# Attention and mixture of experts on one core: the order inside an attention step, the routing chain and the expert loops

## The reference

```python
def xattn(x, context, Wq, Wk, Wv):          # x is layernorm(x)
    q = x @ Wq.T
    k_raw, v_raw = context @ Wk.T, context @ Wv.T
    kv = jnp.concatenate([k_raw, v_raw], -1).reshape(b, m, 32, 16, 2)
    k, v = kv[..., 0].transpose(0, 2, 1, 3), kv[..., 1].transpose(0, 2, 1, 3)
    q, k = rmsnorm(q heads), rmsnorm(k)
    attn = softmax(einsum('bhnd,bhmd->bhnm', q, k) * 16 ** -0.5)
    return einsum('bhnm,bhmd->bhnd', attn, v)   # back to (b, n, 512)

def ffn(x, ...):                            # x is layernorm(x)
    gate = x @ Wr + br
    ids = top_k(gate + gate_bias, 2)
    probs = softmax(gate over the two chosen, -inf elsewhere)
    u = x @ Wup[e] + bup[e]                 # for each of 7 routed experts
    g = silu(u @ Wgate[e] + bgate[e]) * u
    out = sum_e probs[e] * (g @ Wdown[e] + bdown[e])
    return out + the same form with the shared expert's weights

x = x + xattn(layernorm(x), ctx, ...)
x = x + ffn(layernorm(x), ...)
```

## Time and profile before

| | us |
|---|---|
| median of 3 runs | 982.45 |
| range of the runs | 982.33 to 983.61 |
| the profiled execution | 984.33 |
| its span | 982.6 |
| busy: PE / PEld | 952.8 (97%) / 685.5 (70%) |
| busy: DVE / ACT / POOL | 707.1 (72%) / 497.6 (51%) / 203.3 (21%) |
| granted TensorE clock, mean | 0.992 |
| DMA | 86.28 MB, mean 88 GB/s |

### The profile page before, as it was taken

How to read it: one execution, slowest core, us unless ns; L and a number is a source line. 1 busy time by engine, 2 the same in 40 slices (tenths; PEclk the granted TensorE clock), 3 DMA queues, 4 the chain that set the end, 5 groups by cost and what they waited for, 6 DMA issues and landing times.

```text
span 982.6 us, 18038 instructions
## 1 busy us (share of the span) xinstructions
PE 952.8 (97%) x6720; PEld 685.5 (70%) x6721; DVE 707.1 (72%) x1460; ACT 497.6 (51%) x619; POOL 203.3 (21%) x209
## 2 busy tenths in 40 slices
PE   7999999999999999999999999999999999999995
PEld 6633443454443553345989998999989999999995
DVE  6798667876778757885968985855857576858653
ACT  4588568866787568887333222422424243424221
POOL 1011000311012200321100000333233333233331
PEclk9999999999999999999999999999999999999998
DMA  9400100100201020223411242543644536635523
GB/s 331 163 1 22 65 1 1 44 33 12 86 2 43 38 71 1 83 79 102 189 66 44 75 156 97 159 109 53 177 83 103 143 76 190 183 66 152 120 52 41
DMA packets 32217, 86.28 MB, mean 88 GB/s; under 512 B 7712, under 2 KB 7712, under 8 KB 28064
## 3 DMA queue, kind: packets, MB, share of 16 engines
q1 hardware_dynamic: 21632, 59.65, 16.9%
q0 software_dynamic: 10528, 25.87, 13.1%
HBM read 61.83 MB, written 23.67 MB: 87 GB/s over the span
## 4 chain that ended last, share of the span: by engine, by line
PE 85%; DVE 10%; issue 2%; DMA 1%; ACT 1%; DVEq 0%; POOLq 0%; SPq 0%; POOL 0%; ACTq 0%
PE z_ps L875 16%; PE y_ps L875 15%; PE u_ps L875 15%; PE o_ps L611 10%; PE scores L595 7%; PE bank_b L632 5%; PE bank_a L648 4%; PE bank_b L618 2%; PE xt_ps L887 2%; PE bank_a L618 2%; PE tr L671 2%; PE tr L666 1%; PE tr L677 1%; DMA ctx_raw<-ctx_t 1%; DVE k_lo L1390 1%
## 5 line engine op out<-in xcount | busy, mean ns | idle before, releaser
L1144 ACT ACTIVATE probs<-scores 128x2048 f32<-128x2048 f32 x128 | 240.7, 1880 | 77.6 <-PE scores L595 74.6
L875 PE MATMUL z_ps<-u_hi,w_sb 128*128 128x256 f32 x896 | 167.9, 285 | 1.4 <-DVE u_lo L1819 1.4
L875 PE MATMUL u_ps<-x_hi,w_sb 128*128 128x256 f32 x864 | 159.4, 283 | 3.0 <-issue 3.0
L1174 ACT ACTIVATE u_hi<-u_ps,b_ug 128x256 fp32r<-128x256 f32 x108 | 45.4, 471 | 199.9 <-PE u_ps L875 199.9
L875 PEld LDWEIGHTS z_ps<-u_hi,w_sb 128*128 128x128 f32 x896 | 140.6, 190 | 2.7 <-DVE u_lo L1819 1.8
L875 PE MATMUL y_ps<-w_sb,g_hi 128*128 128x512 f32 x448 | 139.5, 392 | 0.0
L875 PEld LDWEIGHTS u_ps<-x_hi,w_sb 128*128 128x128 f32 x864 | 135.5, 190 | 5.5 <-issue 4.5
L611 PE MATMUL o_ps<-probs,v_sb 128*17 128x512 f32 x1024 | 136.4, 605 | 0.0
L875 PE MATMUL z_ps<-u_lo,w_sb 128*128 128x256 f32 x448 | 126.3, 282 | 0.0
L875 PE MATMUL u_ps<-x_lo,w_sb 128*128 128x256 f32 x432 | 121.9, 282 | 0.0
L1186 ACT ACTIVATE s_sb<-z_ps,b_ug 128x256 f32<-128x256 f32 x112 | 47.1, 472 | 105.7 <-PE z_ps L875 105.7
(11 more groups left out here) (246 smaller groups left out, 1579.6 us busy)
## 6 DMA issues: line engine op xcount, KB each, us to landing
w_raw<-w_all SPq DMA_DIRECT2D x27, 1024.0 KB, 6.9
ctx_raw<-ctx_t SPq DMA_DIRECT2D x4, 1024.0 KB, 7.3
out<-x_sb SPq DMA_DIRECT2D x16, 256.0 KB, 2.0
x_sb<-x SPq DMA_DIRECT2D x1, 3072.0 KB, 16.2
xn<-x_t SPq DMA_DIRECT2D x12, 256.0 KB, 4.4
xn_dram<-xn SPq DMA_DIRECT2D x12, 256.0 KB, 2.1
xt_dram<-xt SPq DMA_DIRECT2D x6, 512.0 KB, 3.0
xg<-xt_dram POOLq DMA_DIRECT2D x10, 256.0 KB, 3.2
```

The costliest lines, as they stand in the source:

```text
L875: ins = nc.tensor.matmul(out_ps, stat[a], mov[b], start=(first and a + b == 0), stop=(last and a == 1), skip_group_check=True)
L1144: nc.scalar.activation(probs[:, t % 2], scores[:], ACT.Exp).then_inc(p_ready, 1)
L1174: last = nc.scalar.activation(u_hi[:, c, :], u_ps[:, b, a, :], ACT.Identity, bias=b_ug[:, par, 0, c:c + 1])
```

## The change

1. `weighed(t-1)` comes directly behind `scored(u, s)`, `between` and `after` behind it.
2. In units 2, 6 and 10 `sum_k(u + 1)` moves from `between` of step 2 to `after`, behind v_even; DVE's v_out moves ahead of its sums_k accordingly.
3. PE, ACT and DVE run the seven experts unrolled in Python (`experts`), each with its tile loop; the seven bounds are loaded once into registers, on PE in the y phase of tiles 5 and 6, on ACT and DVE in during_y of tile 7. SP and POOL keep `routed`.
4. SP loads the weights of expert 2 in three pieces (`load_weight`), behind output tiles 5, 13 and 15.
5. One of the splits of the shared expert's down weights goes to ACT (`first_weight_high(2, 3)`, step 7 of unit 13), and DVE's neighbouring ones move: (2,1) to step 6 of unit 13, (2,2) to step 2 and the low part of (2,3) to step 3 of unit 14.
6. Routed y: DVE multiplies the bias by the share ahead of y_ready, in two operations, and one operation for each half (scalar_tensor_tensor) replaces the two behind y_ready.
7. The routing chain on DVE, before -> after: split(1,1,0) tile 3 -> tile 2 during_u; hot_rows(0) tile 4 during_u -> during_y; hot_cols(0) tile 4 during_y -> tile 5 during_u; hot_rows(1) tile 4 -> tile 5 during_y; hot_cols(1) tile 5 during_y -> tile 6 during_u; split(1,1,1) tile 5 during_u -> tile 6 during_y; last_split tile 6 -> tile 7 during_u.

```diff
+        def experts(engine, start_at, head, tile, first_tile=None):
+            for j in range(1, ER + 1):
+                head(j, j % 2, j // 2)
+                first = start_at[j - 1]
+                if first_tile is not None:
+                    first_tile(j, first + NA, j % 2)
+                    first = first + 1
+                with engine.Fori(first, start_at[j]) as i:
+                    tile(i + NA, j % 2, j)
+
+        def bound(engine, e):
+            return engine.value_load(start_i[0:1, e:e + 1], min_val=0, max_val=MOST)
...
+            def load_weight(j, m):
+                sp.wait_ge(lo_done, j * 6 + 2 * m - 10)
+                sp.dma_start(w_raw[:, m], w_all[j, :, m]).then_inc(raw_loaded[m], 16)
...
-                elif t == 11:
-                    sp.wait_ge(lo_done, 6)
-                    load_weights(2)
+                elif t in (5, 13, 15):
+                    load_weight(2, (5, 13, 15).index(t))
...
-                    if u + 1 < UNITS:
+                    if u + 1 < UNITS and not (more and g == 2):
                         sum_k(u + 1)
...
                 if s == 2 and more and g == 2:
                     v_even(u)
+                    sum_k(u + 1)
...
                     scored(u, s)
-                    between(u, s)
                     if u or s:
                         weighed(STEPS * u + s - 1)
+                    between(u, s)
                     after(u, s)
...
+                    if c < len(bounds):
+                        start_at.append(bound(pe, bounds[c]))
...
+            tile(5, 0, behind_up=lambda: table_part(5, 0), windows=2, bounds=range(1, DC + 1))
+            tile(6, 0, behind_up=lambda: table_part(6, 1), windows=3, bounds=range(DC + 1, ER + 1))
...
-            routed(pe, head, tile)
+            experts(pe, start_at, lambda j, par, nth: pe.wait_ge(lo_done, j * 6), tile)
...
-                    if more and g == 3:
+                    if more and g >= 2:
                         v_out(b + 1, 2 * g - 4)
                     if nxt:
                         sums_k(u + 1)
-                    if more and g == 2:
-                        v_out(b + 1, 2 * g - 4)
...
+                    for h in range(2):
+                        nc.vector.tensor_scalar(y_sb[:, h, :], bd[:, par, :], row_now[:, h, j - 1:j], None, ALU.mult)\
+                          .then_inc(y_biased, 1)
...
-                        nc.vector.tensor_scalar(at, at, share, None, ALU.mult).then_inc(y_scaled, 1)
+                        nc.vector.scalar_tensor_tensor(at, y_v[:, h, :], row_now[:, h, j - 1:j], at, ALU.mult,
+                                                       ALU.add).then_inc(y_done, 1)
...
-            tile(4, 0, x_tile=8, during_u=lambda: hot_rows(0),
-                 during_y=steps_of(lambda: hot_cols(0), lambda: hot_rows(1)))
-            tile(5, 0, x_tile=10, during_u=splits(1, 1, [1]), before_x=lambda: table_out(0), during_y=lambda: hot_cols(1))
+            tile(4, 0, x_tile=8, during_y=lambda: hot_rows(0))
+            tile(5, 0, x_tile=10, during_u=lambda: hot_cols(0), before_x=lambda: table_out(0),
+                 during_y=lambda: hot_rows(1))
...
+            tile(7, 0, x_tile=14, during_u=last_split, during_y=bounds)
```

More of the change, by code:

```diff
@@ L912, in table_part, with tile @@
                 last.then_inc(window_ready, 1)
-            def tile(n, par, j=0, behind_up=None, amid_z=None, behind_z=None, windows=0):
+            def tile(n, par, j=0, behind_up=None, amid_z=None, behind_z=None, windows=0, bounds=()):
                 w = w_sb[par]
@@ L973, in _ @@
             tile(4, 0)
-            tile(5, 0, behind_up=lambda: table_part(5, 0), windows=2)
-            tile(6, 0, behind_up=lambda: table_part(6, 1), windows=3)
+            start_at = [0]
+            pe.wait_ge(start_ready, 1)
+            tile(5, 0, behind_up=lambda: table_part(5, 0), windows=2, bounds=range(1, DC + 1))
+            tile(6, 0, behind_up=lambda: table_part(6, 1), windows=3, bounds=range(DC + 1, ER + 1))
             for n in range(7, NA):
                 tile(n, 0)
-            def head(j, par, nth, first):
-                pe.wait_ge(lo_done, j * 6)
-                pe.sem_inc(passed)
-            routed(pe, head, tile)
+            experts(pe, start_at, lambda j, par, nth: pe.wait_ge(lo_done, j * 6), tile)
         @block.scalar
@@ L1201, in _, with bounds, head @@
             tile(3, 0, during_z=choice_exp, during_y=splits(1, 1, [2]))
-            for n in range(4, NA):
+            for n in range(4, NA - 1):
                 tile(n, 0)
-            def head(j, par, nth, first):
+            start_at = [0]
+            def bounds():
+                act.wait_ge(start_ready, 1)
+                for e in range(1, ER + 1):
+                    start_at.append(bound(act, e))
+            tile(NA - 1, 0, during_y=bounds)
+            def head(j, par, nth):
                 act.wait_ge(b_loaded[par], nth * 32 + 32)
@@ L1220, in first_tile @@
                     tile(n, par, before_u=one, during_z=lambda: split(j + 1, 1 - par, 1, [0]), during_y=rest)
-            routed(act, head, tile, first_tile)
+            experts(act, start_at, head, tile, first_tile)
         @block.vector
@@ L1852, in tile @@
                     else:
-                        share = row_now[:, h, bass.ds(j - 1, 1)] if not isinstance(j, int) else row_now[:, h, j - 1:j]
-                        nc.vector.tensor_scalar(at, at, share, None, ALU.mult).then_inc(y_scaled, 1)
+                        nc.vector.scalar_tensor_tensor(at, y_v[:, h, :], row_now[:, h, j - 1:j], at, ALU.mult,
+                                                       ALU.add).then_inc(y_done, 1)
+                        dve.wait_ge(y_done, n * 2 + (h + 1))
+                        dve.sem_inc(y_scaled)
                 if x_tile is None or n == NA - 1:
@@ L1887, in last_split, with bounds, head @@
                 split(1, 1, 2)
-            tile(6, 0, x_tile=12, during_u=last_split, before_x=lambda: table_out(1))
-            for n in range(7, NA):
-                tile(n, 0, x_tile=2 * n)
-            def head(j, par, nth, first):
+            tile(6, 0, x_tile=12, during_u=lambda: hot_cols(1), before_x=lambda: table_out(1),
+                 during_y=splits(1, 1, [1]))
+            start_at = [0]
+            def bounds():
+                dve.wait_ge(start_ready, 1)
+                for e in range(1, ER + 1):
+                    start_at.append(bound(dve, e))
+            tile(7, 0, x_tile=14, during_u=last_split, during_y=bounds)
+            def head(j, par, nth):
                 dve.wait_ge(b_loaded[par], nth * 32 + 32)
-                dve.sem_inc(passed)
             def first_tile(j, n, par):
-                if isinstance(j, int):
+                if j == ER:
                     tile(n, par, j)
@@ L1906, in first_tile @@
                          during_z=lambda: split(j + 1, 1 - par, 1, [0]), during_y=rest)
-            routed(dve, head, tile, first_tile)
+            experts(dve, start_at, head, tile, first_tile)
 def kernel(**inputs):
```

27 lines of the change are left out of this document (14 added, 13 removed).

## The result

| | before | after |
|---|---|---|
| median, us | 982.88 (4 runs) | 989.32 (4 runs) |
| range | 982.33 to 983.61 | 987.27 to 991.23 |
| ratio | | 1.0065, 95% interval 1.0043 to 1.0086 |
| profiled execution / span | 984.33 / 982.6 | 987.27 / 985.5 |
| granted clock, mean | 0.992 | 0.996 |

The change makes the kernel slower by 6.4 us, where the forecast had it 1.4 faster (981.1); the median is 2.3 above the top of the forecast range (973 to 987).

What follows compares the result with a forecast made beforehand. PE, with 85% of the chain, was taken to set the time. Attention +0.2 and FFN -1.6 gave -1.4: profiled 984.33 becomes 983.0, and with 1.9 taken off the median is 981.1, range 973 to 987.

Steps and rivals of the forecast that it cites:

- The views and the bound: Whole kernel: PE's order sets the time; stalls are priced by interval excess over gap-free steps, in the FFN by PE's idle.
- Part 1 (a): Attention, sum_q into step 0: logarithm holds exp 0, so scores 1 come later; +0.68 in six units, +4.3 in all.
- Part 1 (b): Attention, sum_k and step 3: exp 3 held behind a logarithm, +0.51 in regular units, +3.4; units 0 and 1, +1.4.
- Part 2: Units 2, 6, 10: v_even fills PE's idle before sum_k, scores 1 to 4 take 12.4; -7.6 if slow-clock stretches vanish.
- (c): Attention: scores 2 of ten units no longer wait 0.10 for copies, and units 14 and 15 gain 0.3; -1.3.
- Part 3: FFN routing chain: stall at 543.10 goes, -1.05; PE waits 1.0 for hot_cols in tiles 5 and 6, +2.1.
- Part 4: Routed FFN, unrolled loops: PE's issue idles go, -2.5; DVE's bound loads only move its lateness, +0.3.
- Part 5: Routed y, bias ahead of the product: one operation less behind each y half, on the path only at the end; -0.4.
- part 6: Weights 2 loaded and split earlier, one operation moved to ACT: behind other work, 0; bound 0 to +1.
- Rivals. 1 and 2: 1: the attention holds don't come, 973, chance 0.12; 2: the FFN's new waits don't come, 977, chance 0.11.
- Rival 3: Some 20 new PE idles of 0.5 to 1.6 bring the clock to the 1.2 GHz level; up to 988, chance 0.15.
- Rival 4: Parts don't do what they say: PE's bound loads stall it, up to +5.6, 986; chance 0.05.

Runs made afterwards that it cites:

- a_gates: Changed kernel with between ahead of weighed only in step 7 of units 6, 7, 10 and 11; 986.2, ratio 1.0030.
- b_order: Kernel before with only the order changed, weighed ahead of between; 989.4, ratio 1.0063.
- a_bounds: Changed kernel with DVE's seven bound loads spread, two each in during_z of tiles 4 to 6, one in tile 7; 987.9, ratio 1.0058.
- a_xg: Changed kernel with SP's 3 MB weight load waiting until the gather for the expert's third tile has landed; 984.7, ratio 1.0019.
- after_again: Changed kernel run once more as it is; 989.7, ratio 1.0068.
- b_part2: Kernel before with only sum_k behind v_even in units 2, 6, 10 and v_out ahead of sums_k; 975.6, ratio 0.9926.
- best3: best2 with the 3 MB weight load also waiting for the gather; 968.3, ratio 0.9855.
- mended_order: best3 with weighed ahead of between again; 981.75, ratio 0.9995.
- a_loadbounds: Changed kernel with expert 2's third weight piece behind output tile 13 and DVE's bound loads spread; 988.5, ratio 1.0061.
- a_hots: Changed kernel with hot_cols moved behind hot_rows in during_y of tiles 4 and 5; 986.9, ratio 1.0047.
- best2: best1 with expert 2's third weight piece issued early; 973.0, ratio 0.9903.
- a_oldorder: Changed kernel with between ahead of weighed again in every step; 975.0, ratio 0.9915.
- best1: Changed kernel with between ahead of weighed everywhere, hot_cols in during_y of tiles 4 and 5, DVE's bound loads spread; 972.7, ratio 0.9895.
- a_load: Changed kernel with expert 2's third weight piece issued behind output tile 13; 990.0, ratio 1.0074.
- a_logk: Changed kernel with log_k behind exp 3 and root_k one step later on ACT; 994.7 in its one execution.

## Why the prediction was wrong, step by step

**How the miss adds up.** The sum gave 983.0 for the profiled execution, which took 987.27, 4.3 more. Attention is 4.4 of it and the wait for xg 2.1; the time before the first scores is 0.7 shorter (it lies between 32.6 and 33.8 in the traces, so this is scatter) and the rest of the FFN 1.5 shorter than forecast. The median, 989.32 for 981.1, missed by 8.2; the other 3.9 are the offset.

**The views and the bound** held: PE sets the end, and interval excess against twins found every stall of before.

**Part 1 (a)** was right. Step 0 is 0.67 to 0.74 longer in units 3, 4, 5, 9, 13, 14, together 4.2 (forecast 4.1). The 0.12 in 8 and 12 did not come, and step 0 of 7 and 11 is 0.3 shorter than before, where I had put 0; a_gates has that too, so the gates' wait isn't its reason; the reason stays open.

**Part 1 (b)** was right in mechanism and somewhat small: 0.59 a unit instead of 0.51. With units 0 and 1 it is 5.7 against 4.8.

**The step that failed** is in part 1 (a): "In 8 and 12 gates follow the sum, +0.12 each". I priced gates as cover for what comes behind them, and did not ask what they wait for themselves: the buffer that sum_q has just filled. Before, weighed stood between the two, which is longer than the 0.84 missing. It cost 0.91 four times, 3.7, for which the sum had nothing; a_gates gave it back whole (3.5 to 3.8 in the traces, 3.5 in the medians). My own rule, that every instruction moved past a queue counts, was applied to ACT's queue and not to the buffer tr. This is the largest error in attention; the missing term and the offset, below, are the other two that count.

**Part 2** was right: 12.50, 12.48 and 12.48 for 12.4, and the two stretches at clock 0.50 vanished with the idle ahead of them (7.5 of the 7.6). b_order shows that this gain wasn't part 2's alone: the order takes 6.5 of it too. In the sum that did no harm; in the reading of b_order it did.

Attention in all: 4.6 longer (forecast 0.2), 4.4 more than forecast: the gates 3.7, (b) 0.9, step 0 of 7, 8, 11 and 12 0.9 less, and 0.8 in small pieces. Of these 0.3 stands in (c) and in part 2 at once, since scores 1 to 4 of units 2, 6 and 10 hold the 0.10 of (c) too.

**Part 3** right: -0.88 for the stall at 545.83, +1.78 for the tables (forecast 2.1).

**Part 4**: on PE right, the three issue idles are gone and nothing else is. The Trainium skill (Runtime: NRT & Kernel Launch, section Instruction fetch mechanics) has a taken branch stall only if its target isn't in the two pages then loaded. The prediction left that condition out when it let each back branch cost. A routed tile is 128 matmuls and 128 weight loads here, and its back branches show no issue idle on PE in either kernel; whether their targets were loaded the traces don't tell, so the rule is neither borne out nor refuted. What the idles held is in PE's sequencer: the loads of the bounds, 0.30 each and 0.65 to 0.8 with their register work, stand in them. DVE's loads took 4.2 instead of 5.7. u_lo comes 5.2 after PE's first routed matmul (5.3 before), so DVE's lateness was indeed only moved; the stall behind it stayed 0.55, where I had added 1.1. That this helped the sum is luck.

**Part 5** has no run of its own. From the first matmul of the last tile to the end it is 28.2 instead of 28.9, 0.7 less (forecast 0.4).

**The missing term** belongs behind part 4. I followed DVE's lateness to PE and stopped there. It also reaches SP's last output store, POOL's first scatter, which waits for all stores, and the next gather, which waits for the scatter. The last stores leave with PE's first routed matmul in the kernel before and 3.3 behind it in the changed one. The index copy in POOL's timeline, of the kernel before and of the changed one:

```profile
623.34 0.19 POOL L391 COPY index<-table 128x2 int32 x1 [4.05 <-DMA out<-y_sb,target]
```

```profile
630.44 0.43 POOL L405 COPY index<-table 128x2 int32 x1 [4.13 <-DMA out<-y_sb,target]
```

That is 12.8 behind PE's first routed matmul and 16.0 behind it. DVE's lateness is not the whole reason for it: with the bounds spread the last stores leave 2.4 earlier, but the index copy comes only 0.3 earlier (a_bounds). By itself that was harmless: PE asks 24.6 behind that matmul, and a_xg is as late and waits for nothing. But the gather now runs beside 3 MB of weights that used to leave after it. The sum had no term for that: part 6, "behind other work, 0", looked at the weights of expert 2 alone, and the 3 MB are expert 3's, issued 20 behind that matmul in both kernels. Price: 2.06 in the profile, 5.0 in the medians (a_xg against after_again).

**The offset.** I took 1.9 off the profiled sum, since the profiled execution of before stood 1.9 above the median. But that execution holds the two stretches at clock 0.50 that part 2 had already taken out of the sum, so I took a part of this time off twice. In the five kernels whose trace has neither such a stretch nor a long wait for xg (b_part2, b_order, a_xg, best3, mended_order) the profiled execution lies within 0.4 of the median. Besides, after the change the profiled executions were the shortest of theirs (987.27 of up to 991.2, 986.4 of up to 990.2). That scatter goes with the wait for xg, since a_xg has none; that the wait is longer in the executions without a trace is inferred from that and not seen.

**Rivals.** 1 and 2 are refuted by the waits. Rival 3 had the right sign and a wrong mechanism: the clock stayed at 0.996 or 0.997 with 21 holds in b_order. Where it did fall in the trace of a kernel with the change's entry, it was at the wait for xg, an idle that the rival did not have. Rival 4's loads on PE cost nothing.

**Left open**: why the index copy stays 3 late with the bounds spread. In a_bounds POOL gets past the last stores 5.3 after their issue (3.5 in the kernel before). Its copies take 0.18 mostly, but 0.6 to 1.0 in a_bounds and a_loadbounds and 0.95 in a_xg, at times when DVE splits weights. Nothing was run to tell that apart.

## What to carry to other kernels

When two matmul groups swap, look for the third that used to follow them: a group that reuses a buffer needs the time that its neighbour took. When an edit makes one engine late, follow the lateness through every queue to the transfers that it starts, and ask which large transfer starts at a fixed time beside them. A small gather is protected by one wait in front of the large load, which here could be late by 3.8 (638.20 for 634.42) without any wait for its weights.

## What the hardware showed

- The two indirect transfers of a gather of 256 rows landed in 3.5 to 3.7 (median of the two) when 3 MB of plain loads left behind them (before, a_xg, best3), and in 5.5 to 5.6 beside these loads (after_again, a_hots, a_bounds, a_loadbounds, best2).
- Inside the work, the granted clock fell to 0.50 for 3.4 or more only at the end of or right behind PE idles of 1.58 and more: at two of the three of 1.57 to 1.58 in the kernel before, and at the wait for xg of 2.8 to 3.5 in a_oldorder, a_gates, best1, best2, a_load, a_loadbounds and a_logk. Seven idles of 1.57 and more had none (1.57 in the kernel before; 1.63 and 1.66 in a_logk; 1.8, 2.06, 2.71, 3.16 for xg in after_again, after, a_bounds, a_hots), and none of the 21 holds of up to 1.0 in b_order had one. The spread of the kernel before goes with the clock: 979.6 to 982.5 at clock 0.996 or 0.997, 982.8 to 986.6 at 0.990 to 0.994.
- Seven value loads on DVE, none in a loop, held it idle for 4.2, 0.6 each: 0.31 for the load, the rest for register work.
